# Normalised rows stored by the attention stage instead of made in the expert tiles

## The reference

```python
x = x + tanh(g_xattn) * masked_softmax(ln(x) @ ctx^T / sqrt(512)) @ ctx
probs = softmax(ln(x) @ Wg)                  # 8 experts
e = argmax(probs)                            # one expert for each of the 3584 rows
x = x + tanh(g_ffn) * probs[e] * (ln(x) @ W[e] + b[e])
```

## Time and profile before

| | |
|---|---|
| median of 3 runs | 391.01 us |
| the profiled execution, its span | 390.84 us, 388.8 us |
| busy PE, DVE, ACT, POOL | 92%, 77%, 57%, 59% of the span |
| one batch's DMAs on SP's queue | x 224 KB, context 672 and 78 KB, store of x2 224 KB, weight chunk 256 KB |
| moved by DMA, 150 to 195 us | 204 GB/s, DMA engines 84% busy |
| mean granted clock of PE | 0.977 of full speed |

### The profile page before, as it was taken

How to read it: one execution, slowest core, us unless ns; L and a number is a source line. 1 busy time by engine, 2 the same in 40 slices (tenths; PEclk the granted TensorE clock), 3 DMA queues, 4 the chain that set the end, 5 groups by cost and what they waited for, 6 DMA issues and landing times.

```text
span 388.8 us, 9613 instructions
## 1 busy us (share of the span) xinstructions
PE 359.6 (92%) x2062; PEld 303.1 (78%) x2063; DVE 300.9 (77%) x1087; ACT 221.2 (57%) x488; POOL 228.7 (59%) x482
## 2 busy tenths in 40 slices
PE   7799999999999999999999897796999999999980
PEld 6688888888888888888878786674887877878860
DVE  4668888898899899899989887646877767767760
ACT  3577776777777677777767664622444344444410
POOL 5154765666666666665656565736566566666731
PEclk9999999999999999999999998996999999999996
DMA  7958878878989978889866954843355444445410
GB/s 188 235 165 237 189 185 225 204 191 209 220 186 195 227 190 229 194 205 227 189 171 173 249 150 123 230 125 95 123 165 163 152 140 139 142 136 157 143 51 0
DMA packets 39442, 67.26 MB, mean 173 GB/s; under 512 B 10578, under 2 KB 11094, under 8 KB 39416
## 3 DMA queue, kind: packets, MB, share of 16 engines
q1 hardware_dynamic: 32600, 50.35, 52.1%
q0 software_dynamic: 6624, 16.58, 13.8%
q10 hardware_dynamic: 192, 0.03, 0.0%
HBM read 51.68 MB, written 17.10 MB: 177 GB/s over the span
## 4 chain that ended last, share of the span: by engine, by line
PE 54%; DMA 12%; DVE 11%; issue 7%; POOL 5%; SPq 5%; ACT 2%; POOLq 1%; DVEq 1%; ACTq 0%
PE read_both L1160 9%; DMA ctx_sb<-in_ctx 8%; PE read_both L1161 8%; PE ctx_ps L1101 8%; PE score_ps L1195 4%; PE score_ps L1197 4%; PE score_ps L1196 4%; POOL out_rows L605 4%; PE score_ps L1126 3%; PE score_ps L1123 3%; PE score_ps L1124 3%; PE score_ps L1125 3%; PE prob_ps L1110 2%; PE ctx_ps L1181 2%; DMA x_sb<-mid_rows,take 2%
## 5 line engine op out<-in xcount | busy, mean ns | idle before, releaser
L1160 PE MATMUL read_both<-ctx_sb 125*112 125x264 f32 x192 | 61.6, 403 | 0.3 <-ACT ctx_sb L685 0.3
L528 POOL DMA_INDIRECT token_list<-pay,pos x32 | 32.3, 1010 | 47.8 <-DVE pos L902 47.3
L988 DVE TENSOR_TENSOR ctxT_lo<-ctx_ps,ctxT_hi 128x375 fp32r<-128x375 f32 x96 | 49.3, 541 | 13.3 <-ACT ctxT_hi L635 13.0
L1195 PE MATMUL score_ps<-w_hi,ctxT_hi 128*128 x140 | 59.2, 423 | 0.0
L1161 PE MATMUL read_both<-ctx_sb 125*112 125x256 f32 x192 | 57.6, 382 | 0.0
L1101 PE MATMUL ctx_ps<-ident,ctx_sb 125*128 125x125 f32 x384 | 53.0, 273 | 4.2 <-DMA ctx_sb<-in_ctx 2.4
L1197 PE MATMUL score_ps<-w_lo,ctxT_hi 128*128 x140 | 56.1, 401 | 0.0
L1196 PE MATMUL score_ps<-w_hi,ctxT_lo 128*128 x140 | 56.0, 400 | 0.0
L596 POOL DMA_INDIRECT x_sb<-mid_rows,take x35 | 34.4, 982 | 30.8 <-DVE ctx_sb L942 12.0
L605 POOL DMA_INDIRECT out_rows<-ctx_sb,put x35 | 41.3, 1180 | 16.8 <-issue 9.4
L1101 PEld LDWEIGHTS ctx_ps<-ident,ctx_sb 125*128 125x128 f32 x384 | 43.1, 143 | 6.5 <-DVE ctxT_lo L988 2.4
(11 more groups left out here) (141 smaller groups left out, 818.9 us busy)
## 6 DMA issues: line engine op xcount, KB each, us to landing
ctx_sb<-in_ctx SPq DMA_DIRECT2D x32, 672.0 KB
w_raw<-in_L_ffn_W SPq DMA_DIRECT2D x32, 256.0 KB, 4.7
x_sb<-in_x SPq DMA_DIRECT2D x32, 224.0 KB, 3.5
mid_rows<-x SPq DMA_DIRECT2D x32, 224.0 KB, 2.8
ctx_sb<-in_ctx SPq DMA_DIRECT2D x32, 78.0 KB
ctx_sb<-in_L_ffn_b SPq DMA_DIRECT2D x8, 256.0 KB, 4.8
li<-token_list SPq DMA_DIRECT2D x35, 2.0 KB
x_sb<-mid_rows,take POOLq DMA_INDIRECT x35, 3.4
```

The costliest lines, as they stand in the source:

```text
L988: dve.tensor_tensor(ctxT_lo[:, k, 0:M], ctx_ps[k % 2][:, 0:M], ctxT_hi[:, k, 0:M].bitcast(F32), ALU.subtract).then_inc(ctxT_ok, 1)
L1160: pe.matmul(read_a, turned[:, 0:S], turned[:, S:SE + HALF], start=(c == 0), stop=(c == MC - 1))
L1195: pe.matmul(y_ps[a][:, :], hi, w_hi[:, chunk], start=(k == 0), stop=False)
```

## The change

ScalarE normalises x2 in place during attention (`apply2`, after the statistics), and that is what `keep` stores. So TensorE turns the gathered rows themselves, and `rn` is gone. For the residual, ScalarE rebuilds x2 from the gathered rows beside that (`restore`, with the row's std and mean, into `base`), and VectorE adds the bias there. The record in the list therefore carries std and mean; GpSimd makes them in `stats2` with five more small operations. SyncE's batch issues the loads of batch i+4 on `x2_ok`, and the store of batch i-1 behind them on the new `xh_ok`. At the end the stores stand one place later, and lists 4 to 7 are loaded ahead of the last store.

```diff
@@ sync
             def keep(i):
-                sp.wait_ge(x2_ok, i.times(1, 1))
+                sp.wait_ge(xh_ok, i.times(1, 1))
                 sp.dma_start(mid[bass.ds(i.times(S), S), :], x2[:, i.slot(2), :]).then_inc(mid_st[i.slot(2)], 16)
             def batch(i):
                 next_w(i)
-                keep(i)
+                sp.wait_ge(x2_ok, i.times(1, 1))
                 load(i.plus(4))
+                if i.at_least(1):
+                    keep(i.plus(-1))
...
             next_w(Count(B - 4))
+            keep(Count(B - 5))
+            next_w(Count(B - 3))
             keep(Count(B - 4))
-            next_w(Count(B - 3))
...
+            for t in range(4, 2 * TURN):
+                load_list(Count(t))
             keep(Count(B - 1))
-            for t in range(4, EARLY):
+            for t in range(2 * TURN, EARLY):
                 load_list(Count(t))
@@ gpsimd, stats2
+                if j.at_least(2):
+                    pool.wait_ge(lsum_ok, j.times(1, -1))
+                    pool.wait_ge(xh_ok, j.times(1, -1))
...
-                pool.tensor_tensor(pay[:, b, 2:3], ve2[:, a, 0:1], half[0:S, :], ALU.pow).then_inc(rs2_ok, 1)
+                pool.tensor_tensor(ln2[:, a, 0:1], ve2[:, a, 0:1], half[0:S, :], ALU.pow).then_inc(rs2_ok, 1)
...
-                pool.tensor_tensor(pay[:, b, 3:4], ve2[:, a, 1:2], pay[:, b, 2:3], ALU.mult).then_inc(nm2_ok, 1)
+                pool.tensor_tensor(ln2[:, a, 1:2], ve2[:, a, 1:2], ln2[:, a, 0:1], ALU.mult).then_inc(nm2_ok, 1)
+                pool.tensor_tensor(std2[:, 0:1], ve2[:, a, 0:1], ln2[:, a, 0:1], ALU.mult).then_inc(std2_step, 1)
+                pool.tensor_tensor(pay[:, b, 3:4], ve2[:, a, 1:2], minus[0:S, :], ALU.mult).then_inc(mean2_ok, 1)
+                pool.wait_ge(std2_step, j.times(3, 1))
+                pool.tensor_tensor(std2[:, 1:2], std2[:, 0:1], ln2[:, a, 0:1], ALU.mult).then_inc(std2_step, 1)
+                pool.wait_ge(std2_step, j.times(3, 2))
+                pool.tensor_tensor(std2[:, 2:3], two[0:S, :], std2[:, 1:2], ALU.subtract).then_inc(std2_step, 1)
+                pool.wait_ge(std2_step, j.times(3, 3))
+                pool.tensor_tensor(pay[:, b, 2:3], std2[:, 0:1], std2[:, 2:3], ALU.mult).then_inc(std2_ok, 1)
@@ scalar
-            def normal(t):
+            def restore(t):
                 act.wait_ge(row_ld[t.slot(4)], t.rounds(4) * 16 + 16)
                 if t.at_least(2):
-                    act.wait_ge(rnT_mm, t.times(1, -1))
-                act.activation(rn[:, t.slot(2), :], rows[:, t.slot(4), :], ACT.Identity,
+                    act.wait_ge(y_ok, t.times(1, -1))
+                else:
+                    act.wait_ge(w_lo_ok, B)
+                act.activation(base[:, t.slot(2), :], rows[:, t.slot(4), :], ACT.Identity,
                                bias=..., scale=...)
             def tile(t):
                 turned_rows(t)
-                if t.plus(1).within(TILES):
-                    normal(t.plus(1))
+                restore(t)
...
+            def apply2(j):
+                a = j.slot(2)
+                act.wait_ge(rs2_ok, j.times(1, 1))
+                act.wait_ge(nm2_ok, j.times(1, 1))
+                act.activation(x2[:, a, :], x2[:, a, :], ACT.Identity, bias=ln2[:, a, 1:2], scale=ln2[:, a, 0:1]
+                               ).then_inc(xh_ok, 1)
... (at the end of batch(i))
+                if i.plus(-1).within(B):
+                    apply2(i.plus(-1))
@@ vector, finish
+                    dve.wait_ge(back_ok, t.times(1, 1))
-                    dve.scalar_tensor_tensor(rows[:, b, :], biases..., rows[:, b, :], ALU.mult, ALU.add)
+                    dve.scalar_tensor_tensor(base[:, a, :], biases..., base[:, a, :], ALU.mult, ALU.add)
@@ tensor, turn_rows
-                    pe.wait_ge(rn_ok, t.times(1, 1))
+                    pe.wait_ge(row_ld[t.slot(4)], t.rounds(4) * 16 + 16)
...
-                        last = pe.transpose(row_ps[a][:, k * P:(k + 1) * P], rn[:, a, k * P:(k + 1) * P], ident[:, :])
+                        last = pe.transpose(row_ps[a][:, k * P:(k + 1) * P], rows[:, t.slot(4), k * P:(k + 1) * P], ident[:, :])
```

More of the change, by code:

```diff
@@ L162, in build @@
         minus = sb("minus", [P, 1])
+        two = sb("two", [P, 1])
         token_ids = sb("token_ids", [P, B], I32)
@@ L206, in build @@
         ve2 = sb("ve2", [S, 2, 2])
+        ln2 = sb("ln2", [S, 2, 2])
+        std2 = sb("std2", [S, 3])
         std1 = sb("std1", [S, 4, 1])
@@ L253, in build @@
         rows, biases, res = x_sb, ctx_sb[:, 0:E, SE:], ctx_sb[:, E:E + 4, SE:]
-        rn = sb("rn", [P, 2, D])
+        base = w_raw
         rnT_hi, rnT_lo = (part[:, :, :].rearrange("p k m -> p (k m)")[:, 0:2 * D].rearrange("p (a d) -> p a d", a=2)
@@ L291, in build @@
         const = sem("const")
-        pad_ok, nm2_ok = sem("pad_ok"), sem("nm2_ok")
+        pad_ok, nm2_ok, std2_ok, mean2_ok, xh_ok = (sem(n) for n in ("pad_ok", "nm2_ok", "std2_ok", "mean2_ok", "xh_ok"))
+        two_ok, std2_step = sem("two_ok"), sem("std2_step")
         mask_clear, ident_ok, select_ok = sem("mask_clear"), sem("ident_ok"), sem("select_ok")
@@ L318, in build @@
         rnT_hi_ok = sem("rnT_hi_ok")
-        take_ok, put_ok, rn_ok, rnT_mm, rnT_ok, base_ok, y_mm, y_ok = (
-            sem(n) for n in ("take_ok", "put_ok", "rn_ok", "rnT_mm", "rnT_ok", "base_ok", "y_mm", "y_ok"))
+        take_ok, put_ok, back_ok, rnT_mm, rnT_ok, base_ok, y_mm, y_ok = (
+            sem(n) for n in ("take_ok", "put_ok", "back_ok", "rnT_mm", "rnT_ok", "base_ok", "y_mm", "y_ok"))
         CONSTS = 14
@@ L461, in _ @@
             pool.memset(minus[:, :], -1.0).then_inc(const, 1)
+            pool.memset(two[:, :], 2.0).then_inc(two_ok, 1)
+            pool.wait_ge(two_ok, 1)
             if ME > M:
@@ L525, in file @@
                 pool.wait_ge(scale_ok, now)
-                pool.wait_ge(nm2_ok, now)
+                pool.wait_ge(std2_ok, now)
+                pool.wait_ge(mean2_ok, now)
                 filing.begin(j)
@@ L637, in ctx_part @@
                     act.activation(ctxT_full[:, 0:M], ctx_ps[k % 2][:, 0:M], ACT.Copy).then_inc(ctxT_full_ok, 1)
-            def normal(t):
+            def restore(t):
                 act.wait_ge(row_ld[t.slot(4)], t.rounds(4) * 16 + 16)
                 if t.at_least(2):
-                    act.wait_ge(rnT_mm, t.times(1, -1))
-                act.activation(rn[:, t.slot(2), :], rows[:, t.slot(4), :], ACT.Identity,
+                    act.wait_ge(y_ok, t.times(1, -1))
+                else:
+                    act.wait_ge(w_lo_ok, B)
+                act.activation(base[:, t.slot(2), :], rows[:, t.slot(4), :], ACT.Identity,
                                bias=li[:, bass.ds(t.times(1), 1), 3:4].rearrange("p o c -> p (o c)"),
-                               scale=li[:, bass.ds(t.times(1), 1), 2:3].rearrange("p o c -> p (o c)")).then_inc(rn_ok, 1)
+                               scale=li[:, bass.ds(t.times(1), 1), 2:3].rearrange("p o c -> p (o c)")).then_inc(back_ok, 1)
             def tile(t):
                 turned_rows(t)
-                if t.plus(1).within(TILES):
-                    normal(t.plus(1))
+                restore(t)
             def turned_rows(t):
@@ L705, in choice_weights @@
                 act.wait_ge(rs2_ok, j.times(1, 1))
-                act.activation(lexp[:, :], lsh[:, j.slot(2), :], ACT.Exp, scale=pay[:, j.slot(4), 2:3],
+                act.activation(lexp[:, :], lsh[:, j.slot(2), :], ACT.Exp, scale=ln2[:, j.slot(2), 0:1],
                                accum_out=lsum[:, j.slot(2):j.slot(2) + 1]).then_inc(lsum_ok, 1)
@@ L739, in batch @@
                         weights(ahead)
+                if i.plus(-1).within(B):
+                    apply2(i.plus(-1))
             run(act, -2, B - 2, batch, loop_to=TAIL)
-            normal(Count(0))
             choice_weights(Count(B - 4))
@@ L750, in _ @@
             turned_rows(Count(0))
-            normal(Count(1))
+            apply2(Count(B - 3))
             choice_weights(Count(B - 3))
             turned_weights(Count(B - 1))
+            restore(Count(0))
             turned_rows(Count(1))
-            normal(Count(2))
+            apply2(Count(B - 2))
             choice_weights(Count(B - 2))
+            restore(Count(1))
             turned_rows(Count(2))
+            act.wait_ge(lsum_ok, B - 1)
             choice_weights(Count(B - 1))
-            normal(Count(3))
+            apply2(Count(B - 1))
+            restore(Count(2))
             run(act, 3, TILES, tile)
@@ L936, in finish @@
                     expert = dve.value_load(tile_expert[0:1, bass.ds(t.times(1), 1)], min_val=0, max_val=E - 1)
-                    dve.scalar_tensor_tensor(rows[:, b, :], biases[:, bass.ds(expert, 1), :].rearrange("p o d -> p (o d)"),
+                    a = t.slot(2)
+                    dve.wait_ge(back_ok, t.times(1, 1))
+                    dve.scalar_tensor_tensor(base[:, a, :], biases[:, bass.ds(expert, 1), :].rearrange("p o d -> p (o d)"),
```

(4 more changed lines are left out.)

## The result

The changed kernel takes 419.68 us (median of 4 runs, 418.49 to 423.12) against 390.98 us before in the same comparison: ratio 1.075, 95% interval 1.068 to 1.082. Slower by 29 us; 416.2 was forecast. The profiled execution is the one of 418.49 us, with a span of 416.5. Ratios and intervals leave out executions in a slower state, among the experiments above all one of the four with four buffers (607.63 us, granted clock 0.557) and two of the four with the order alone (432.75 and 434.93 us).

A forecast was written before the change was run, and what follows sets the result against it. Attention was taken as bound by TensorE and the DMA engines at once, 7.34 us a batch. 390.84 + 28.2 (store behind loads) - 3 (tiles and turn) = 416.0 us, median about 416.2, range 396 to 436.

The forecast's parts named there:

- The deciding step: Attention: store behind loads on SyncE's queue makes residual wait; 8.47 us a step against 7.34, 28.2 us over 25 steps.
- the store lands in time: Attention: the store's landing is hidden, residual never waits, L under 6.4 us; 387 us in all, chance 0.11.
- Tiles and turn: After attention: TensorE's waits for normalised rows shrink (2.5 us), VectorE's wait for list 4 too (0.5); sum -3 us.
- apply2 and GpSimd's five operations, costed at 0: Attention: apply2's 0.81 us fits ScalarE's 0.95 us wait; GpSimd's 1.3 us fits ahead of the filing; cost 0.
- the sign on record: Attention, ScalarE: its wait before L700, the normalisation of x, gone would show the forecast right.
- The term of GpSimd: Attention: five small operations, 1.3 us a batch, ahead of split and filing, which waited 1.34 us; cost 0, at most 0.1.
- The clock rival: Attention: TensorE, idle some 1.2 us a batch, drops its clock in a third of periods; +40, 456 us, chance 0.03.
- signs of being wrong: Attention: L837 7.2 us apart without store wait, landing under 6.4 us, xn late, or clock below 1.00 before 230 us.
- The sum: Whole kernel: 390.84 + 28.2 - 3 = 416.0 us for the profiled execution, median about 416.2.

The follow-up runs named there:

- four buffers: The changed kernel with four buffers of x2 instead of two, so the residual waits for the store of j-3: 400.45 us, ratio 1.017.
- the order alone: The kernel before with one edit, SyncE issuing the loads of batch i+4 first and the store of x2(i-1) behind them: 430.38 us.
- the better of the last two kernels: The changed kernel with the store ahead of the loads, GpSimd's split early, and lists 4 to 7 and bias loads early: 387.97 us, ratio 0.991.

## Why the prediction was right, point by point

*The deciding step held.* The loop over residual, load issues and store was forecast with L = 7.5 us from x's issue to the store's landing and 8.47 us a step. From x's issue to the store's are 2.4 us (119.28 to 121.68), the median landing is 5.0 us later, so L = 7.4, and the steps are 8.51. 28.2 us were forecast for the steps, 29.2 came. The order alone gives the slowdown; waiting for a store one batch older, another place and another queue each take the wait for it away or nearly so, and most of the loss with it.

*The rival "the store lands in time"* needed L under 6.4 us; the shortest of the 25 that the residual waited for was 6.9. The Trainium skill's fit (DMA: Bandwidth & Descriptors, section Anatomy of one DMA), 2.0 us plus bytes at 436 GB/s, by which it would have come true at an estimated 4.8, doesn't hold for 1.2 MB in four pieces behind each other here: measured 7.4. The page gives that fit for one DMA that GpSimd issues, so the prediction took it beyond what it says.

*Tiles and turn.* -3 forecast, -1.9 measured, and that it came so near is in part luck: two errors stand against each other. From the first product on the gain is 4.4 us instead of some 2.5. TensorE's waits for rn went nearly as said (3.1 to 0.7 us), and VectorE's wait for list 4 fell from 2.47 to 0.80 us, though the last bias loads still stand between the store that waits for apply2 and that list. The turn up to the first product lost 2.5 us, where 0.5 of gain was put. Two of its steps hold that loss. The one to the residual of batch 28 takes 10.5 us instead of 9.7: VectorE waits 3.3 us for the first four lists, 2.3 before. The one from the residual of batch 30 to that of 31 takes 7.9 us instead of 6.4: TensorE works at half clock in it from 283.1 to 286.6, as it doesn't in the kernel before. In the better of the last two kernels the early lists and biases took away VectorE's wait for list 4, but its step to the residual of batch 31 is 7.9 us long too.

*apply2 and GpSimd's five operations, costed at 0.* No run shows a cost of apply2, and none measures it alone; of ScalarE's wait before xn 14.3 us remained, where the sign on record was that it goes. The term of GpSimd was wrong as a statement and unpunished, by luck: I asked only whether its own queue had room (1.34 us before the filing), and not what the shifted split would meet on another engine. In the changed kernel VectorE waits for the store anyway, and in 18 batches acc starts 0.2 us before the split, so that its mean is only 287 ns; with the store's wait gone the collision costs 5 to 8 us.

*The clock rival* came in a small part, and with it one of the signs of being wrong, a granted clock below 1.00 before 230 us. The steps contain two spells of half clock, 6.8 us together. One lies inside a period that the store sets; behind the other TensorE comes last, in a step of 8.34 us, which is under the mean. My bound was "1.71 us of idle time left the clock alone", and it doesn't hold; see below. Nor does the prediction list the idle time of 2.40 us before 237.51 in the kernel before, behind which TensorE ran at half clock too (0.50 from 237.8 to 241.2).

*The sum* is 3.5 us under the median. 1.2 of it is that the profiled execution lies under the median of its runs (418.49 and 419.68); of the 2.5 us between 416.0 and 418.49 the steps have 1.0, the turn with the tiles 1.1 and the start 0.4.

## What to carry to other kernels

A store that frees one of two buffers must not stand behind the loads on its queue: its latency then contains theirs, and where the next producer waits for it, the period becomes their sum. Before moving an issue, write down which instruction waits for its landing and how many periods it has. And when small operations are put ahead of a long one on GpSimd, look up which of VectorE's instructions the long one will now run beside.

## What the runs showed of the hardware

A VectorE instruction of 0.15 us with two inputs in SBUF took up to 1.28 us when it started inside a GpSimd instruction of 1.27 us that reads two as well.

The store of 224 KB landed 2.8 to 3.3 us (medians of the kernels) after its issue ahead of the loads, 5.0 to 6.1 us behind 974 KB of them on the same queue, and 4.2 to 4.7 us beside them on ScalarE's queue.

TensorE's clock fell to the lower of its two levels behind an idle time of 1.87 us and again behind one of 1.71 us in the changed kernel. One of 1.71 us had left it alone in the kernel before, and one of 1.81 us left it alone in the kernel with the order alone. So the length of a single idle time doesn't tell these cases apart. The timeline of TensorE in the changed kernel, and the windows around the two idle times (us, PE, PEld, DVE, ACT, POOL, granted clock, DMA share, GB/s):

```profile
87.21 0.21 PE L1184 MATMUL small_ps<-acc,ones_bf 128*112 128x8 bf16 x1 [1.87 <-DVE hot L921]
...
138.17 0.21 PE L1184 MATMUL small_ps<-acc,ones_bf 128*112 128x8 bf16 x1 [1.71 <-DVE hot L921]
```

```profile
84.00:88.60 4.60, 2.73 (x21) 2.23 (x20) 3.86 (x16) 1.94 (x6) 1.58 (x8) 1.00 0.29 82
88.60:92.00 3.40, 3.40 (x14) 2.91 (x13) 2.69 (x12) 2.60 (x6) 2.98 (x7) 0.50 0.86 257
...
136.40:139.80 3.40, 1.69 (x13) 1.43 (x13) 3.36 (x19) 1.50 (x5) 1.74 (x9) 0.99 0.45 116
139.80:143.20 3.40, 3.40 (x12) 2.78 (x11) 2.37 (x10) 3.08 (x7) 3.22 (x7) 0.50 0.95 277
```

In the second and the fourth stretch TensorE ran at 1.2 instead of 2.4 GHz although it was busy throughout. The same for the kernel with the order alone:

```profile
193.44 0.21 PE L1149 MATMUL small_ps<-acc,ones_bf 128*112 128x8 bf16 x1 [1.81 <-DVE hot L888]
```

```profile
190.00:194.00 4.00, 2.19 (x16) 1.70 (x15) 3.01 (x15) 2.14 (x6) 1.00 (x5) 1.00 0.23 64
194.00:198.00 4.00, 4.00 (x27) 3.51 (x25) 3.62 (x14) 3.00 (x8) 2.61 (x5) 1.00 0.98 270
```
